# Delta-memory attention: probabilities turned two tiles at a time, local products in four quarters of TensorE

## What is computed

```python
def step(carry, seg):
    mem, z = carry
    qq, kk, vv = seg
    sigma_q = jax.nn.elu(qq) + 1.0
    scores = jnp.einsum('bhsk,bhtk->bhst', qq, kk) / scale
    scores = jnp.where(causal_mask, scores, -jnp.inf)
    att_dot = jax.nn.softmax(scores, axis=-1) @ vv
    att_mem = sigma_q @ mem / (sigma_q @ z)
    sigma_k = jax.nn.elu(kk) + 1.0
    delta = vv - sigma_k @ mem / (sigma_k @ z)
    mem_new = mem + jnp.einsum('bhsk,bhsv->bhkv', sigma_k, delta)
    z_new = z + sigma_k.sum(axis=-2, keepdims=True).transpose(0, 1, 3, 2)
    att = beta * att_mem + (1.0 - beta) * att_dot
    out = att.reshape(Bsz, SEG, H * DV) @ Wo
    return ((mem_new, z_new), out)
```

## Time and profile before

| | |
|---|---|
| median of 3 runs | 678.33 us (678.25 to 682.52) |
| the profiled execution | 681.31 us |
| its span, from the first to the last instruction | 679.3 us |
| PE busy over the span | 620.1 us (91%) |
| DVE, ACT, POOL busy | 407.5, 375.2, 172.2 us |
| stages 1 to 6 of the attention | 51.0 to 51.2 us each |

### The profile page before, as it was taken

One profiled execution on the slowest core, in us unless ns is written; L12 is line 12 of the kernel. 1 busy time (PEld: TensorE's weight loads), 2 busy tenths in 40 slices (PEclk: granted clock), 3 DMA queues, 4 the chain that ended last, 5 costly groups with the idle time before them and its releaser, 6 DMA issues. The chain is left out here.

```text
span 679.3 us, 12696 instructions
## 1 busy us (share of the span) xinstructions
PE 620.1 (91%) x4390; PEld 523.8 (77%) x4390; DVE 407.5 (60%) x1057; ACT 375.2 (55%) x882; POOL 172.2 (25%) x189
## 2 busy tenths in 40 slices
PE   3999999999999999999999998697999958996796
PEld 3878888988988988988988988586455546985553
DVE  6757595196396196396196273768445479535554
ACT  2679769479569479569469464222466521201242
POOL 4702011011011011011011021342477514301454
PEclk9999999999999999999999999899999978998799
DMA  8200200000120000100000051298233261008631
GB/s 265 78 2 1 81 14 1 3 6 2 34 68 1 2 6 1 32 6 0 5 5 1 3 123 40 73 408 314 62 95 101 73 238 69 0 1 307 235 91 35
DMA packets 25459, 48.99 MB, mean 72 GB/s; under 512 B 4062, under 2 KB 15296, under 8 KB 25408
## 3 DMA queue, kind: packets, MB, share of 16 engines
q1 hardware_dynamic: 19456, 35.74, 15.2%
q0 software_dynamic: 3840, 10.49, 5.1%
q10 hardware_dynamic: 2112, 2.10, 0.9%
HBM read 40.06 MB, written 8.78 MB: 72 GB/s over the span
## 5 line engine op out<-in xcount | busy, mean ns | idle before, releaser
L932 DVE RECIPROCAL denominators<-readings 128x2 f32<-128x2 f32 x128 | 21.3, 167 | 143.8 <-PE readings L572 143.4
L572 PEld LDWEIGHTS readings<-memory_copy,sigma 128*128 128x128 f32 x512 | 75.3, 191 | 11.7 <-ACT memory_copy L779 2.6
L788 ACT ACTIVATE memory_reading<-readings,denominators 64x128 f32<-64x128 f32 x256 | 78.5, 356 | 5.3 <-DVE denominators L932 3.3
L572 PE MATMUL readings<-memory_copy,sigma 128*128 128x129 f32 x512 | 78.7, 275 | 2.6 <-ACT memory_copy L779 2.5
L779 ACT ACTIVATE memory_copy<-memory 128x258 f32<-128x258 f32 x128 | 50.1, 392 | 55.4 <-PE memory L582 40.9
L938 DVE SCALAR_TENSOR_TENSOR minus_delta<-readings,denominators,v 64x128 f32<-64x128 f32 x240 | 73.8, 347 | 4.5 <-DVE denominators L932 0.3
L582 PE MATMUL memory<-minus_delta,sigma_k_tokens 128*128 128x129 f32 x480 | 73.2, 275 | 0.0
L481 POOL TENSOR_TENSOR xn<-scores,exp_sum_inverse 64x512 f32<-64x512 f32 x32 | 33.8, 1055 | 133.8 <-DVE exp_sum_inverse L959 132.6
L472 POOL TENSOR_TENSOR scores<-scores,score_max 128x512 f32<-128x512 f32 x16 | 16.7, 1044 | 195.3 <-DVE score_max L953 195.3
L621 PE MATMUL ahead<-wo,attT 128*128 128x256 f32 x256 | 64.5, 396 | 1.0 <-DVE attT L967 1.0
L582 PEld LDWEIGHTS memory<-minus_delta,sigma_k_tokens 128*128 128x128 f32 x480 | 63.0, 191 | 0.0
(11 more groups left out here) (303 smaller groups left out, 1465.1 us busy)
## 6 DMA issues: line engine op xcount, KB each, us to landing
weights_e<-experts SPq DMA_DIRECT2D x24, 608.0 KB, 12.5
xn<-L_attn_Wq SPq DMA_DIRECT2D x4, 512.0 KB, 4.0
wo<-L_attn_Wo SPq DMA_DIRECT2D x1, 2048.0 KB, 12.9
rows_e<-xn ACTq DMA_DIRECT2D x4, 512.0 KB, 10.8
carried<-L_attn_Wk SPq DMA_DIRECT2D x3, 512.0 KB, 4.8
xn<-L_attn_Wv SPq DMA_DIRECT2D x3, 512.0 KB, 4.0
x<-L_attn_x SPq DMA_DIRECT2D x4, 256.0 KB, 3.5
x<-L_attn_x SPq DMA_DIRECT2D x2, 512.0 KB, 3.5
```

What stands on the lines that cost most here:

```text
L572: last = pe.matmul(KQ[g][:, hh * MC:(hh + 1) * MC], sqk[:, GROUP * g + hh, pair, 2 * par:2 * par + 2, :], mz[g][:, hh, :], start=True, sto ...
L788: last = act.activation(read[rows, half, GROUP * g + hh, pair, :], KQ[g][rows, hh * MC:hh * MC + DK], ACT.Copy, scale=nr[g][rows, hh:hh + 1])
```

## The change

- `probs` loses its zeros: 64 columns a tile, one POOL instruction over all 128 partitions instead of two over 64. One transpose now takes two tiles (128 columns), so `turn_probs` has 4 transposes for two heads instead of 8.
- The turned pair stands in PSUM with keys of the even and the odd tile on different halves, so the copy to `pTs` is done in four blocks of 64 partitions x 128 elements for each head; ACT copies those of the first head, DVE (a new `copy_probs` on its stream) those of the second.
- `local` is made of 64 x 64 quarters of the array: for each head, tile and segment two products (two halves of the value columns), 32 for two heads instead of 8 full ones. The even segments' products go to bank `L[0]`, the odd ones' to `L[1]`. It moves behind `project` in slot 10 and behind `project_out` in slot 14; its wait for the copies moves to before the last three matmuls of that projection, or to before that `project_out`. `scale_local` reads from both banks.
- In slot 9 ACT copies sigma of k before the exponential and the copy of the probabilities, instead of behind them.
- The memory's seed is a bfloat16 matmul (one record) instead of a float32 one (two), with a bfloat16 identity that POOL makes once at the start.
- In three places without a projection in front of `local` (slot 10 of the last stage, slot 14 of the first and the last) one 128 x 128 transpose (`busy`) stands before it.

```diff
+        banks_local = ctx.enter_context(nc.psum_tensor("local", [P, 2 * HALF], F32))[:, :]
+        L = [banks_local[:, i * HALF:(i + 1) * HALF] for i in range(2)]
...
+        def blocks_of_probs(hh):
+
+            turned = L[hh][:, 0:HALF // 2].rearrange("p (j c) -> p j c", c=P)
+            by_tile = pTs[hh].rearrange("p (j b c) -> p j b c", b=2, c=SEG)
+            return [(by_tile[par * SEG:(par + 1) * SEG, :, b, :],
+                     turned[b * SEG:(b + 1) * SEG, :, par * SEG:(par + 1) * SEG]) for b in range(2) for par in range(2)]
...
-                    for par in range(2):
-                        rows = slice(par * SEG, (par + 1) * SEG)
-                        pool.tensor_tensor(probs[rows, :, par * SEG:(par + 1) * SEG], sm[rows, :, :],
-                                           rs[rows, :].unsqueeze(2).to_broadcast([SEG, NT, SEG]), ALU.mult)\
-                            .then_inc(p_ready, 1)
+                    pool.tensor_tensor(probs[:, :, :], sm[:, :, :], rs[:, :].unsqueeze(2).to_broadcast([P, NT, SEG]),
+                                       ALU.mult).then_inc(p_ready, 1)
...
                     for k in range(KD):
+                        if k == KD - 1 and probs_of is not None:
+                            wait_probs(*probs_of)
...
-                    pe.matmul(MM[g][:, 0:GROUP * MC], ident[:, :], start[:, :], start=True, stop=True,
+                    pe.matmul(MM[g][:, 0:GROUP * MC], ident_16[:, :], start[:, :], start=True, stop=True,
...
                 def turn_probs(n, pp, hh):
-                    for t in range(TPH):
-                        last = pe.transpose(L[hh][:, t * P:(t + 1) * P], probs[:, hh * TPH + t, :], ident[:, :])
+                    for t in range(0, TPH, 2):
+                        two = probs[:, hh * TPH + t:hh * TPH + t + 2, :].rearrange("p t c -> p (t c)")
+                        last = pe.transpose(L[hh][:, t // 2 * P:(t // 2 + 1) * P], two, ident[:, :])
                     last.then_inc(pT_ready, 1)
...
+                def local(n, half, pp):
+
+                    for hh in range(GROUP):
+                        for t in range(TPH):
+                            for par in range(2):
+                                keys = slice(par * SEG, (par + 1) * SEG)
+                                at = (hh * TPH + t) * SEG
+                                for c in range(2):
+                                    begin = (GROUP * pp + hh) * DK + c * SEG
+                                    last = pe.matmul(L[par][c * SEG:(c + 1) * SEG, at:at + SEG],
+                                                     v[keys, half * TPH + t, begin:begin + SEG],
+                                                     pTs[hh][keys, t * SEG:(t + 1) * SEG], start=True, stop=True)
                     last.then_inc(bt_ready, 1)
...
                     if m == 12:
-                        pe.wait_ge(p_ready, 4 * n + 4)
+                        pe.wait_ge(p_ready, 2 * n + 2)
+                        pe.wait_ge(bt_copied, 4 * n + 2)
                         for hh in range(2):
-                            pe.wait_ge(bt_copied, 4 * n + hh + 1)
                             turn_probs(n, 1, hh)
...
                 def copy_probs(n, pp):
-                    for hh in range(2):
-                        act.wait_ge(pT_ready, 4 * n + 2 * pp + hh + 1)
-                        act.activation(pTs[hh][:, :], L[hh][:, :], ACT.Copy).then_inc(pTs_ready, 1)
+                    act.wait_ge(pT_ready, 4 * n + 2 * pp + 1)
+                    for dst, src in blocks_of_probs(0):
+                        last = act.activation(dst, src, ACT.Copy)
+                    last.then_inc(pTs_ready[0], 1)
...
                 def scale_local(n, half, pp):
...
+                        src = banks_local.rearrange("p (a r t c) -> p r t a c", a=2, r=2, c=SEG)[:, hh, :, :, :]
+                        act.activation(by_parity, src, ACT.Copy, scale=one_less_q[:, h:h + 1]).then_inc(bt_copied, 1)
...
+                    if m == 9:
+                        turned_ahead(it, half, m + 1, last)
                     if m in (4, 9):
                         exp_scores(n, m // 8)
...
+                def copy_probs(n, pp):
+                    dve.wait_ge(pT_ready, 4 * n + 2 * pp + 2)
+                    for dst, src in blocks_of_probs(1):
+                        last = dve.tensor_copy(dst, src)
+                    last.then_inc(pTs_ready[1], 1)
```

More of the change, by code:

```diff
@@ L597, in turn_probs @@
                 def turn_probs(n, pp, hh):
-                    for t in range(TPH):
-                        last = pe.transpose(L[hh][:, t * P:(t + 1) * P], probs[:, hh * TPH + t, :], ident[:, :])
+                    for t in range(0, TPH, 2):
+                        two = probs[:, hh * TPH + t:hh * TPH + t + 2, :].rearrange("p t c -> p (t c)")
+                        last = pe.transpose(L[hh][:, t // 2 * P:(t // 2 + 1) * P], two, ident[:, :])
                     last.then_inc(pT_ready, 1)
-                def local(n, half, pp, hh):
-                    h = GROUP * pp + hh
-                    pe.wait_ge(pTs_ready, 4 * n + h + 1)
-                    for t in range(TPH):
-                        last = pe.matmul(L[hh][:, t * P:(t + 1) * P], v[:, half * TPH + t, h * DK:(h + 1) * DK],
-                                         pTs[hh][:, t * P:(t + 1) * P], start=True, stop=True)
+                def local(n, half, pp):
+                    for hh in range(GROUP):
+                        for t in range(TPH):
[7 more added lines that the diff above has]
+                                                     pTs[hh][keys, t * SEG:(t + 1) * SEG], start=True, stop=True)
                     last.then_inc(bt_ready, 1)
@@ L672, in slot @@
                                 free = (skt_copied, 4 * n + 4) if first else (y_copied, n - 1)
-                            project(n + 1, it + half, 1 - half, u, free)
-                    out_at = OUT_AT if ahead else LAST_OUT_AT
+                            project(n + 1, it + half, 1 - half, u, free, probs_of=(n, 0) if m == 10 else None)
+                    if m in (10, 14) and not (ahead if m == 10 else behind and m in out_at):
+                        wait_probs(n, (m - 10) // 4)
+                        busy(pe, L[0], ident, 1)
+                    if m == 10:
+                        local(n, half, 0)
+                    if m == 14 and behind and m in out_at:
+                        wait_probs(n, 1)
                     if behind and m in out_at:
@@ L682, in slot @@
                         project_out(1 - half, out_at[m])
+                    if m == 14:
+                        local(n, half, 1)
                 def turn(it, first, last):
@@ L819, in copy_ahead, with turned_ahead @@
                         for what, u in AHEAD_AT.get(m - 1, ()):
-                            (copy_sigma_k if what == "turn" else copy_projection)(n + 1, 1 - half, u)
+                            if what == "project":
+                                copy_projection(n + 1, 1 - half, u)
+                            elif m != 10:
+                                copy_sigma_k(n + 1, 1 - half, u)
+                def turned_ahead(it, half, m, last):
+                    n = 2 * it + half
+                    if not (last and half):
+                        for what, u in AHEAD_AT.get(m - 1, ()):
+                            if what == "turn":
+                                copy_sigma_k(n + 1, 1 - half, u)
                 def weights_high(it, half, m, last):
```

42 lines of the change are left out of this document (22 added, 20 removed).

## The result

| | before | after |
|---|---|---|
| median of 14 runs each | 680.19 us | 675.52 us |
| ratio, 95% interval | | 0.9922 (0.9907 to 0.9937) |
| span of the profiled execution | 679.3 us | 673.4 us |
| from stage 0's first read to stage 7's last | 381.5 us | 374.8 us |

The change makes the kernel 0.8% faster, where 1.9% was forecast. The time lies inside the stated range. In the profiled executions the eight stages give back 6.7 us, not 13.1, and the rest of the program takes 0.8 us more (6.7 less the 5.9 of the spans).

The account below looks back on a forecast made before the run. PE's issued work was taken to bound the stages, with ACT second in slots 6 to 10. Stages 1 to 6 (8.5), stage 0 (0.7), stage 7 (1.4) and seeds (2.5) sum to 13.1 us: 665.3 us, range 659 to 678.

Parts of the forecast that it names:

- slots 8 to 10, stages 1 to 6: PE's slots 8 to 10: 0.37 us gained a stage, limited by ACT's chain, though PE's own work fell 1.19.
- slot 12: PE's four transposes instead of eight in slot 12: 0.43 us less in each of stages 1 to 6.
- slot 14: Local products as quarters in slot 14: 0.62 us less in each of stages 1 to 6.
- The copies: ACT's four copies of 64 x 128: 0.20 us each, 0.80 together, with bounds 0.12 and 0.245 each.
- the new idle time: PE before slot 10's projection: idle some 1.2 us, waiting for ACT's copy of the values.
- Local block: 64 quarter records, four abreast, instead of 16 full ones: 1.16 us a block, saving 0.62.
- The rival built on the 25 ns: Local block bound by issue pace, 1.60 to 2.26 us; median 672.2 to 682.8 us; chance 0.23.
- Transposes: Four transposes of the probabilities instead of eight: 0.43 us less, twice a stage.
- 0.1 us to spare: Slot 12: ACT's scalings end near 219.7, PE arrives at 219.8, so the turn need not wait.
- Seeds: Memory seed as one pass instead of two records of two passes: 0.31 us less, eight times, 2.5 us.
- Stages 0 and 7: First and last stage: 0.7 us saved in stage 0, 1.4 in stage 7.
- ACT eats more: DVE not relieved: slots 8 to 10 lose 0.20 us, slot 12 waits 0.1; 669.3 us; chance 0.14.

Follow-up runs that it names:

- dve_copies: The changed kernel with DVE making all eight copies of the probabilities and ACT none: 666.70 us, ratio 0.9796 to the kernel before.
- split_copies: The changed kernel with ACT copying sigma of k, values, two of eight probability copies, then exponential; DVE makes six: 663.13 us, 0.9737 of before.
- sigma_last: The changed kernel with ACT copying slot 9's sigma of k behind the probabilities again: 674.68 us, ratio 0.9921 to the kernel before.
- local_first: The changed kernel with slot 10's wait and local products ahead of turn and projection, one transpose in front: 675.34 us, ratio 0.9922 to before.
- local_twice: The changed kernel with every local block made twice in a row, 128 records instead of 64: 691.83 us, ratio 1.0176 to the kernel before.
- seed_float32: The changed kernel with the memory's seed in float32 again, two records a seed: 677.61 us, ratio 0.9954 to the kernel before.
- pool_halves: The changed kernel with POOL's multiplication as two instructions of 64 partitions again: 678.88 us, ratio 0.9983 to the kernel before.
- pe_unrolled: The changed kernel with PE's loop over the turns written out: 674.13 us, ratio 0.9927 to the kernel before.

## Why the prediction was wrong

Its sum, beside what the slots show in the traces of before and after:

| term | forecast | measured |
|---|---|---|
| slots 8 to 10, stages 1 to 6 | 6 x 0.37 = 2.2 | 0.0 |
| slot 12 | 6 x 0.43 = 2.6 | 2.0 |
| slot 14 | 6 x 0.62 = 3.7 | 3.6 |
| seeds (slots 0 of stages 0, 2, 4, 6; slots 15 of 1, 3, 5) | 2.5 | 1.1 |
| stage 0, slots 1 to 14 | 0.7 | -0.3 |
| stage 7, slots 1 to 14 | 1.4 | 0.6 |
| slot 7, stages 1 to 6 | not seen | 0.9 |
| slot 0 of stage 1 | not seen | -0.5 |
| slots 15 of stages 0, 2, 4, 6 | not seen | -0.4 |
| slot 11 and the other slots | 0 | -0.3 |
| sum | 13.1 | 6.7 |

**The copies (failed, the largest step).** The step that failed is the price of ACT's four copies, taken as 0.20 us each. The mechanism of slots 8 to 10 was forecast as it came: DVE relieved, slot 8 shorter by 0.57, PE idle in slot 10 until ACT's copy of the values. The size was not. From slot 9's update the chain was to take 4.81 us to the projection; it took 5.15 (207.17 to 212.32). The copies account for it: 1.13 us instead of 0.80, that is 0.283 each, outside the bounds of 0.12 to 0.245. The scaled reading in the earlier trace rows has the same shape, but not the same price; as an upper bound it was an operation that merely looked alike, and no row spoke for the 0.20 between the bounds. What makes the difference between 0.245 and 0.283 I did not test. The other pieces of the chain were within 0.11 and cancelled: 1.71 instead of 1.60 to sigma of k, 0.52 instead of 0.63 for the exponential. So 0.34 us a stage of the forecast 0.37 went, and dve_copies and split_copies show that this row of ACT holds slot 10. In stages 1 to 6 that is 2.0 of the 6.4 us that are missing; no other single row of the table is as large, but together the others are larger.

**Where the saved PE time goes.** The prediction had the new idle time at 1.2 us, so it knew that ACT would bind in slot 10, and it counted PE's saving there by the end of ACT's chain, rightly. The consequence that it did not draw: what PE is spared between slot 9's update and that wait only makes the wait longer, and each 0.1 us on ACT's row costs 0.1 us (1.13 us taken off the row by dve_copies make slot 10 1.12 shorter). What stands behind the wait still counts in full: with the local block made twice, slot 10 grows by 0.92 to 0.96 us in all stages but one, as slot 14 does by 0.93. sigma_last and local_first, which keep ACT's copies and change the order, do not move the time by more than the intervals.

**Local block (right).** 1.09 us against 1.16 forecast, slot 14 shorter by 0.60 against 0.62. That these two agree so well is in part luck: in stage 3 the block became 0.69 shorter (1.78 to 1.09), and the output projection beside it 0.10 longer (228.33 to 229.31 before, 224.34 to 225.42 now). The Trainium skill, "TensorE: Matmul & The Clock Gate", section "Back-to-back issue gap", gives about 25 ns as the least distance between matmuls of 1 to 64 columns. Across quarters it does not hold here: local_twice shows 14.6 ns. The rival built on the 25 ns gave a time that the result fell into, by a mechanism that did not happen.

**Transposes (right, less one thing).** Four take 0.44 to 0.49 in stages 2 to 6. Slot 12 gave 0.33 instead of 0.43. In stage 3 its transposes start 0.53 us after the update, not 0.45, and take 0.47. The prediction had 0.1 us to spare before ACT's scalings; I read the 0.08 as that wait, though the profile names none: they start 0.14 us behind the end of the scalings (218.20), and as much behind them in local_first (217.72 and 217.86). It also fits that local_first, whose local block and scalings end earlier, has 2.79 there instead of 2.86.

**Seeds (a little mis-sized).** One record takes 0.11 us as forecast, and seed_float32 gives about 2.0 us instead of 2.5: in slots 15 the output projection behind the bfloat16 seed takes 2.76 us (127.62 to 130.38 in stage 1), where behind the float32 one it takes 2.67 (128.86 to 131.53 in seed_float32). In the table only 1.1 shows, since slots 15 also hold the longer read behind the quarters (0.11 in each) and stage 3's jump back (0.46).

**Stages 0 and 7 (mis-sized).** Stage 0 gave nothing: slot 10 lengthened by 0.57 there too, and in slot 14 PE waits 0.6 us for ACT's copies (the longest of the third row of the waits) where the block's saving should stand. Stage 7 saved 0.23, 0.12, 0.23 and 0.34 in slots 8, 10, 12 and 14 and lost 0.10, 0.10 and 0.11 in 9, 11 and 13: the read behind four transposes or a block lasts 0.55 there.

**Not foreseen.** Slot 7 became 0.15 us shorter, and pool_halves takes that back, so it came from DVE's relief too. In slot 0 of stage 1 the scores wait for both scalings of the local products, 0.4 us, the fourth row of the waits; before, stage 1's slot 0 took 3.68 us, now 4.17. The jump back costs 0.46 us in stage 3. The instruction queue moved more, as the queue's lines of the page show, before and then after:

```profile
q8 instruction: 30, 0.49, 0.3%
```

```profile
q8 instruction: 43, 0.70, 0.4%
```

pe_unrolled shows that the 0.46 us belong to the loop. Its queue moved 42 packets without that stall, so the stall goes with the jump and not with the amount fetched. That the longer body (14161 instructions in the program instead of 12696) no longer stays loaded is how I read the 43 packets; it is argued, not shown. The Trainium skill, "Runtime: NRT & Kernel Launch", section "Instruction fetch mechanics", says that a taken branch to a place that isn't loaded stalls for a fetch; the trace agrees with the stall, and no run here shows what is held loaded.

**The other rivals.** "ACT eats more" had the right place but the wrong reason: it wanted DVE not relieved, and pool_halves shows that DVE was, and that this alone carries 4.0 of the 6.7 us. The 0.8 us that the rest of the program took more lie within its scatter: it is the same code before and after, and in the profiles of the fourteen kernels (span less eight stages) it takes between 295.7 and 300.2 us.

## What to carry to other kernels

Where a saving on the bound engine ends in a wait for a second engine, price the second engine's row item by item, and treat an operation of another bank or another access pattern as unknown even if the shape is the same: 0.08 us a copy, four copies ahead of each wait, ate nearly all that slots 8 to 10 were to give (2.0 of 2.2 us). Splitting wide copies into several small ones can make a full engine's row longer although less is copied (0.97 to 1.13 us here); share the pieces with an idle engine, and put ahead what is waited for first. When a change saves much less than the work it removes, look for the one wait that appeared, and shorten the row of the engine that it names up to that point. An order that leaves the same work ahead of it (sigma_last) brings nothing.

## What the runs showed of the hardware

- Four 64 x 64 quarters of TensorE run abreast at 14.6 ns a float32 record, weight loads included, when the stream goes round the quarters (local_twice); with 8 products of a quarter in a row the block takes 3.33 us instead of 1.09.
- Every read behind a block of quarters lasts 0.55 us instead of 0.44. It is no matter of quarters alone: reads behind PE's waits and behind the half-array scores of stage 7 last 0.55 in both kernels. The prediction could have read this from the trace of before, and did not price it.
- Copies of 64 x 128 float32 out of PSUM follow each other at 0.28 us on ACT and 0.305 on DVE; two full 128 x 512 ones on ACT took 0.97 together.
- DVE's sigma of k (128 x 512, two inputs) takes 1.42 us beside POOL's multiplication and 0.69 without it.
- POOL's multiplication takes 1.13 us on 64 partitions (pool_halves) and 1.04 on all 128.
